# A graph-network kernel: basis loads on 96 partitions and 16-bit one-hots for sorting and counting the edges

## What is computed

```python
h = relu(layernorm(x))
x = x + L0(h, edges, node_vec1)      # 4 blocks of sparse attention and MLP, scale and bias of the norms from node_vec1
h = relu(layernorm(x))
x = x + L1(h, edges, edge_type_2)    # 2 relational layers

# attention of a block: softmax over the edges that leave a node
scores = sum(q[src] * k[dst]);  out = segment_sum(softmax(scores) * v[dst], src) @ wo + bo
# relational layer, R = 2 relations, B = 30 bases
w = einsum('rb,bio->rio', att, basis)                  # basis: 30 x 512 x 512
agg[row] += sigmoid(x[col] @ gate_w[r]) * x[col] @ w[r]     # r is the edge's type
out = agg + x @ root + bias
```

## Time and profile before

| | before |
|---|---|
| median of 3 executions | 2405.82 us (2404.52 to 2407.23) |
| profiled execution, its own time | 2413.9 us |
| its span | 2412.1 us |
| PE busy | 2200.1 us (91%) |
| PEld busy | 1886.1 us (78%) |
| DVE busy | 1638.5 us (68%) |
| ACT busy | 1153.2 us (48%) |
| POOL busy | 549.6 us (23%) |
| basis loads | 32 x 1920 KB, median 16.0 us from issue to landing |

### The profile page before, as it was taken

One profiled execution on the slowest core, in us unless ns is written; L12 is line 12 of the kernel. 1 busy time (PEld: TensorE's weight loads), 2 busy tenths in 40 slices (PEclk: granted clock), 3 DMA queues, 4 the chain that ended last, 5 costly groups with the idle time before them and its releaser, 6 DMA issues.

```text
span 2412.1 us, 36415 instructions
## 1 busy us (share of the span) xinstructions
PE 2200.1 (91%) x13669; PEld 1886.1 (78%) x13669; DVE 1638.5 (68%) x3599; ACT 1153.2 (48%) x1826; POOL 549.6 (23%) x402
## 2 busy tenths in 40 slices
PE   2678884899999999999999999999999999999999
PEld 1454443789988888998888999888899888877887
DVE  7989996548877646877754787765588775244234
ACT  4116668337773335775333777433477633322321
POOL 3400000016650003663000665100266400000000
PEclk9899996899999999999999999999999999999999
DMA  7699998211112202003101110320210231031023
GB/s 167 172 220 208 202 224 260 83 51 33 32 36 78 71 19 63 22 22 105 61 29 30 43 43 1 113 71 9 57 37 22 79 105 45 1 112 46 1 67 103
DMA packets 67182, 189.53 MB, mean 79 GB/s; under 512 B 6737, under 2 KB 7185, under 8 KB 66505
## 3 DMA queue, kind: packets, MB, share of 16 engines
q1 hardware_dynamic: 63318, 180.50, 28.0%
q10 hardware_dynamic: 3699, 6.76, 0.9%
HBM read 155.15 MB, written 32.07 MB: 78 GB/s over the span
## 4 chain that ended last, share of the span: by engine, by line
PE 70%; DVE 11%; issue 6%; ACT 6%; DVEq 3%; DMA 3%; SPq 1%; POOL 0%; ACTq 0%
PE PS L1039 10%; PE PS L1067 9%; PE PS L958 6%; PE PS L960 6%; PE PS L959 6%; PE PS L1053 6%; PE PS L944 5%; PE PS L948 4%; PE PS L945 4%; PE PS L1195 4%; PE PS L1205 4%; DVE chunk_hot L1660 2%; DVEq L1696 2%; ACT prob L1423 1%; PE PS L879 1%
## 5 line engine op out<-in xcount | busy, mean ns | idle before, releaser
L785 POOL TENSOR_SCALAR prob<-prob,inv_den 125x1000 f32<-125x1000 f32 x160 | 444.5, 2778 | 0.0
L773 POOL TENSOR_TENSOR rstd<-var_eps,neg_half 125x2 f32<-125x2 f32 x45 | 33.4, 743 | 954.6 <-DVE var_eps L1584 954.6
L1423 ACT ACTIVATE prob<-prob,neg_max 125x1254 f32<-125x1254 f32 x160 | 215.4, 1346 | 56.8 <-DVE neg_max L1916 56.6
L1911 DVE CUSTOM_DVE_ANT_0 prob<-PS,sbias 125x1254 f32<-125x1254 f32 x160 | 233.1, 1457 | 9.8 <-issue 7.1
L1067 PE MATMUL PS<-pT_hi,v_hi 125*128 125x250 f32 x800 | 236.1, 295 | 0.0
L1930 DVE TENSOR_TENSOR pT_lo<-PS,pT_hi 125x1000 fp32r<-125x1000 f32 x160 | 191.1, 1195 | 50.7 <-ACT pT_hi L1440 50.7
L1067 PE MATMUL PS<-pT_lo,v_hi 125*128 125x250 f32 x800 | 224.1, 280 | 0.0
L1067 PE MATMUL PS<-pT_hi,v_lo 125*128 125x250 f32 x800 | 222.4, 278 | 0.0
L1053 PE MATMUL PS<-ident,prob 125*125 125x125 f32 x1600 | 201.1, 273 | 5.6 <-DVE pT_lo L1933 5.6
L1053 PEld LDWEIGHTS PS<-ident,prob 125*125 125x125 f32 x1600 | 195.5, 188 | 12.7 <-issue 7.6
L1438 ACT ACTIVATE pT_hi<-PS 125x1000 fp32r<-125x1000 f32 x160 | 161.8, 1011 | 81.4 <-PE PS L1053 81.4
(11 more groups left out here) (329 smaller groups left out, 5725.2 us busy)
## 6 DMA issues: line engine op xcount, KB each, us to landing
basis_t<-in_L_gnn_basis_dram SPq DMA_DIRECT2D x32, 1920.0 KB, 16.0
sbias<-score_bias SPq DMA_DIRECT2D x40, 548.6 KB
adj<-adj SPq DMA_DIRECT2D x20, 546.9 KB
w_lo_raw<-in_L_gnn_m_w_dram SPq DMA_DIRECT2D x8, 1024.0 KB, 6.8
score_bias<-cnt SPq DMA_DIRECT2D x10, 548.6 KB
adj<-count_t SPq DMA_DIRECT2D x10, 546.9 KB
xc<-x_lat SPq DMA_DIRECT2D x12, 448.0 KB
x_first<-x_lat SPq DMA_DIRECT2D x10, 448.0 KB
```

Source lines behind the costliest of these rows:

```text
L785: pool.tensor_scalar(prob[u % 3][:, 0:SPLIT], prob[u % 3][:, 0:SPLIT], inv_den[0:T, u % 4:u % 4 + 1], None, ALU.mult)\
L1423: act.activation(prob[u % 3][:], prob[u % 3][:], ACT.Exp, bias=neg_max[0:T, u % 4:u % 4 + 1], accum_out=den[0:T, u % 4:u % 4 + 1]).then_in ...
L1911: v.tensor_tensor_reduce(prob[u % 3][:].rearrange("p (j s) -> p j s", j=3), PS[0:T, 0:3, 0:SB], sbias[p % 2][a][:].rearrange("p (j s) -> p ...
```

## The change

- `load_bases` brings 80 loads of 96 partitions (GROUP_B = 6 bases x GROUP_I = 16 rows) x 4 rows, 786 KB each, into RING = 6 buffers; a partition reads its four rows as 8 KB in one piece. Five loads (NBG) make one output bank of 128 rows, with four matmuls each, and `att_z` holds 5 blocks of 32 columns in place of shifted ones. The tables count loads now: 5 first, 2 and 3 in turn in the ten sort batches, one in each second group, one in the first bias tile.
- The sort has 10 batches of 16 chunks. `chunk_hot` is a single 16-bit compare per chunk and carries no code. For the whole batch one compare makes `place_hot` [128, 128 slots, 16 chunks], and two products make `src_place` and `dst_place` from it. PE multiplies each chunk_hot with both (two matmuls a chunk, banks 5 and 4); the stationary operand is `[:, :, i]`, with a step of 16 elements. DVE waits for `x_sums` once, since place_hot shares its bytes with ACT's `sq_junk`.
- `dst_hot` is made for two groups in one compare, [128, 128, 4]; its stationary slices have a step of 4 elements.
- The nine small loads move from SP's queue to ACT's, behind the ten loads of x.
- `load_r` brings each relation matrix in 8 pieces of 64 partitions.

```diff
-    QL = 8
-    SORT_BATCH = 8
+    GROUP_B, GROUP_I = 6, 16
+    NBG = B // GROUP_B
+    GP = GROUP_B * GROUP_I
+    GR = 4 * GROUP_I
+    RING = 6
+    SORT_BATCH = 16
...
-        STEPS_FIRST = 2 * QL
-        QUADS_SORT = [b for b in range(SORT_BATCHES) if b % 10]
-        QUADS_COUNT = [n for n in range(NG) if n % 8 in (1, 4, 7)]
+        LOADS_FIRST = NBG
+        LOADS_SORT = [2 + b % 2 for b in range(SORT_BATCHES)]
+        LOADS_COUNT = [n % 2 for n in range(NG)]
...
-                w = rel_w[l, :, n, :, :] if n < R else (root1, root2)[l].rearrange("(c p) d -> p c d", p=128)
-                sp.dma_start(wr_raw[n][:], w).then_inc(w_in[n].sem, 16)
+                if n == R:
+                    sp.dma_start(wr_raw[n][:], (root1, root2)[l].rearrange("(c p) d -> p c d", p=128)).then_inc(rel_in[n], 16)
+                else:
+                    for k in range(D // GR):
+                        p0 = GR * (k % 2)
+                        sp.dma_start(wr_raw[n][p0:p0 + GR, k // 2, :],
+                                     rel_w[l, k, :, :].rearrange("(j r i) d -> r i j d", j=4, r=R)[n]).then_inc(rel_in[n], 16)
...
             def load_bases(n):
-                l, q0 = divmod(n * QL, Q)
-                if n >= 3:
-                    sp.wait_ge(basis_used, n - 2)
-                rows = (basis1, basis2)[l].rearrange("b (i q k t) d -> (b i) q k t d", i=4, k=4, t=4)
-                t = q0 % 16 // 4
-                sp.dma_start(basis_t[n % 3][:].rearrange("p (k t) d -> p k t d", k=4),
-                             rows[:, q0 // 16, :, t:t + 2, :]).then_inc(basis_in[n % 3], 16)
+                group, g = divmod(n, NBG)
+                l, k = divmod(group, NW // 2)
+                if n >= RING:
+                    sp.wait_ge(basis_used, n - RING + 1)
+                rows = (basis1, basis2)[l].rearrange("(b g) a d -> g b a d", g=NBG)[g][:, GR * k:GR * (k + 1), :]
+                sp.dma_start(basis_t[n % RING][:], rows.rearrange("b (i j) d -> i b (j d)", j=4)).then_inc(basis_in[n % RING], 16)
...
+            def relation_loads(first, count):
+
+                for load in range(first, first + count):
+                    n, g = divmod(load, NBG)
+                    if g == 0 and n >= 2:
                         pe.wait_ge(basis_out, n - 1)
+                    pe.wait_ge(basis_in[load % RING], 16 * (load // RING + 1))
+                    for j in range(4):
+                        mm = pe.matmul(PS[32 * j:32 * (j + 1), 6 + n % 2, :],
+                                       att_z[n // (NW // 2)][:, g, :, :].rearrange("p r i -> p (r i)"),
+                                       basis_t[load % RING][:, j, :], start=(g == 0), stop=(g == NBG - 1))
+                    mm.then_inc(basis_used, 1)
...
-                    g = pe.matmul(PS[:, 5, 0:TC], place_hot[b % 2][:, i, :], chunk_hot[b % 2][:, i, :],
-                                  start=(c == 0), stop=(c == EC - 1))
+                    for bank, place in ((5, src_place), (4, dst_place)):
+                        g = pe.matmul(PS[:, bank, 0:TC], place[b % 2][:, :, i], chunk_hot[b % 2][:, i, :],
+                                      start=(c == 0), stop=(c == EC - 1))
                 g.then_inc(sort_used, 1)
...
-                        g = pe.matmul(PS[0:T, 3 * b + j, 0:SB], dst_hot[b][:, h, 0:T],
+                        g = pe.matmul(PS[0:T, 3 * b + j, 0:SB], dst_hot[n // 2 % 2][:, 0:T, 2 * b + h],
...
+            v.wait_ge(x_sums, 2 * NT + 1)
             for b in range(SORT_BATCHES):
...
-                    v.tensor_scalar(place_hot[b % 2][:, i, :], slot_no[:, 0:128], pos_p[:, c:c + 1], None, ALU.is_equal)
-                    last = v.tensor_scalar(chunk_hot[b % 2][:, i, :], slot_no[:], pos_c[:, c:c + 1], code[:, c:c + 1],
-                                           ALU.is_equal, ALU.mult)
-                last.then_inc(sort_hot, 1)
+                    v.tensor_scalar(chunk_hot[b % 2][:, i, :], chunk_no[:], pos_c[:, SORT_BATCH * b + i:SORT_BATCH * b + i + 1],
+                                    None, ALU.is_equal)
+                if b:
+                    v.wait_ge(sort_hot, b)
+                v.tensor_tensor(place_hot[:], by_slot(edge_place), slot_no[:], ALU.is_equal)\
+                    .then_inc(place_done, 1)
+                v.wait_ge(place_done, b + 1)
+                v.tensor_tensor(src_place[b % 2][:], place_hot[:], by_slot(edge_src), ALU.mult)
+                v.tensor_tensor(dst_place[b % 2][:], place_hot[:], by_slot(edge_dst), ALU.mult).then_inc(sort_hot, 1)
...
+                if b == 0:
+                    v.tensor_tensor(dst_hot[turn][:], slot_no[:, :, 0:4],
+                                    slot_dst[:, bass.ds(4 * it, 4)].unsqueeze(1).to_broadcast([128, 128, 4]), ALU.is_equal)
```

More of the change, by code:

```diff
@@ L826, in _ @@
             pe.wait_ge(att_ready, 2 * R)
-            relation_steps(0, STEPS_FIRST)
-            step = STEPS_FIRST
+            relation_loads(0, LOADS_FIRST)
+            load = LOADS_FIRST
             for b in range(SORT_BATCHES):
@@ L1510, in _ @@
                         o_high(4)
+                    if last and p in (0, 1, 3):
+                        r_high(0, (0, 1, None, 2)[p])
+                    elif p == 0:
                         w_high(wk_hi, wk_raw, 0, lay, 0)
```

241 lines of the change are left out of this document (115 added, 126 removed).

## The result

| | before | after |
|---|---|---|
| median | 2406.53 us (2404.52 to 2408.31) | 2364.73 us (2362.01 to 2368.22) |
| ratio, 95% interval | | 0.9829 (0.9816 to 0.9841) |
| profiled execution, its span | 2413.9, 2412.1 us | 2362.0, 2360.3 us |
| PE, DVE, ACT busy in the counting | 162.2, 191.4, 123.7 of 195 us | 178.4, 174.5, 123.4 of 179 us |

The account below looks back on a forecast made before the run. The prediction took VectorE to bound the setup's sort and counting, and ACT the bias tiles. Its terms, -25.5 - 1 - 15.7 - 3 + 2 = -43.2 us, gave a median of 2362 us, 8 in 10 within 2340 to 2400.

Parts of the forecast that it names:

- sort: Setup's sort: batched 16-bit one-hots and matmuls end it at 137.5 us instead of 163.0, saving 25.5 us.
- counting: Setup's counting: one compare serves two groups, 3.60 us per two groups on VectorE, 180.6 us in all, saving 15.7 us.
- bias tiles: Setup's ten bias tiles: fewer loads ahead of the store of adjacency counts, saving 3 us, between 0 and 11.
- behind: Relation weights at the end: 17 DMAs where 3 were, ahead of adjacency tile 2, costing 2 us, between nothing and 4.8.
- slot table: Table of slots in the setup: five instructions on 196 slots become two, saving 1 us.
- 24.2 us as a stop that remains: In the sort, POOL's z product and memset of count lock out VectorE for 24.2 us, before and after the change.
- The batch of 7.6 us on TensorE: In the sort, 32 matmuls at 0.16 us plus 2.5 basis loads at 0.99 take 7.6 us, over VectorE's 6.5.
- Rival D: POOL's lock in the sort shrinks, its product needing 2.88 us, not 13.47; 10 us more go: 2352 us, chance 0.14.
- Over 260 GB/s, then DMA hides: Setup's new basis loads run at over 260 GB/s, above the 242 needed in the counting, so their DMA is hidden.
- Rival A: Setup's basis loads stay slow at 205 GB/s, so 36 us of the saving go: 2398 us, chance 0.14.
- Rival B: Strided weights slow sort and counting; x, one matmul with its load, decides from 0.25 us: 2425 us, chance 0.10.
- Rival C: Two-input 16-bit compares with a repeated operand run at the 32-bit rate, 2.24 and 0.60 us: 2403 us, chance 0.06.

Follow-up runs that it names:

- e1: The kernel before, unchanged, profiled a second time: 2409.1 us, ratio 1.0001 to the kernel before, span 2403.1 us.
- e4: The changed kernel with the nine small loads back on SP's queue, behind the first six basis loads: 2367.8 us, ratio 0.9827.
- e3: The kernel before with the new basis loads and small relation-weight pieces, but its own sort, one-hots and small loads on SP's queue: 2404.8 us, ratio 0.9986.
- e7: As e6, with two basis loads in every sort batch and the five others in the bias tiles: 2361.1 us, ratio 0.9793.
- e2: The changed kernel with the old basis loads (32 loads of 120 partitions) and three DMAs for the relation weights: 2384.1 us, ratio 0.9887.
- e8: The changed kernel with dst_hot packed as 4 x 128, so its weights are read without a step: 2377.0 us, ratio 0.9854.
- e5: The changed kernel with layer 2's relation weights loaded behind adjacency tiles 2, 3 and 4 instead of ahead of tile 2: 2363.3 us, ratio 0.9802.
- e6: The changed kernel with count cleared on ACT in place of POOL's memset: 2358.3 us, ratio 0.9786.
- e11: The changed kernel with the six bases of a load 1 MB apart in HBM in place of 5 MB: 2367.5 us, ratio 0.9837.
- e10: The changed kernel with the edits of both e5 and e6: 2355.7 us, ratio 0.9784.

## Why the prediction was right

The number came out within 3 us of the median, but partly since errors cancelled: the sort was undersized by 6.8 us, and three other terms together (counting, bias tiles, behind) were too good by 7.0.

| term | forecast | by the spans against e1 |
|---|---|---|
| sort | -25.5 | -32.3 |
| slot table | -1 | -0.9 |
| counting | -15.7 | -13.4 |
| bias tiles | -3 | -1.3 |
| behind (relation weights) | +2 | +5.0 |
| sum | -43.2 | -42.9 |

**The sort.** The batch on VectorE was right: 6.41 us for 6.5. The step that failed inside the right sum is "24.2 us as a stop that remains". It was twice wrong: e1 shows 13.5 for the kernel before, so 163.0 was 8.4 us too late a base, and the changed kernel loses 10.6. So DVE has the second batch ready at 64.5 us, where the forecast had 74: 9.5 of the 15.2 us between 137.5 and 122.3. The other 5.7 come from TensorE: from there the forecast had 63.5 us to the end (nine batches of 7.6, less the short tail), and it took 57.8. Less the 8.4 of the base this makes the 6.8 by which the saving was undersized.

The batch of 7.6 us on TensorE went by 0.16 us a sort matmul. That holds at the lower clock (0.163 apart at 90.3 to 93 us) and not at the full one (0.085 at 121 to 122 us): 196 columns at 1.2 and 2.4 GHz. At full clock TensorE keeps up with VectorE, and until 90 us its batches start 6.41 us apart; the next two take 7.2 and 7.3 us, with matmuls of the noise net (2.3 us) and a stretch at the lower clock in them, and behind them a basis load is last. So TensorE as the limit was right for a part of the sort only, and the place near 122 us is the sum of three limits that no single term of the forecast had.

Rival D had the mechanism: POOL needs 2.8 to 6.0 us for the product in every other trace here, and the 13.47 with a chunk_hot of 10.8 us beside it occurred once. It was given 0.14 and should have had more, as the same shape stood in the profile with 2.88 us. But D put the gain at 10 us of time, and the median did not move with it, since the base moved too.

**The small loads** cost and bring nothing in the changed kernel (e4); the sum had no term of its own for them. But they were part of e1's 10.7 us wait on DVE, and e3 shows that the smaller basis loads ahead of them remove most of it without the move.

**The counting.** 3.60 us for two groups was exact, and the weight load stayed under the matmul, 196 ns under 203. Of the 2.1 us missing much is likely at the start: the three loads behind the last sort batch wait for DMAs until 128.9 us, and DVE then waits 3.2 us for PE, where e1 has 1.9 in all. That isn't shown to be all of it: in e7 no load waits there, and its counting is no shorter (183.8 us).

**The basis loads.** "Over 260 GB/s, then DMA hides" was half right: 257 to 269 with a full queue, enough in the counting, where PE waits for no load from 131 us on, not enough at the end of the sort. Rival A's mechanism is real where its condition holds (e2: 2384 us; A had put 2398), and the change avoids it.

**Rival B** is excluded: x was 0.085 to 0.163, its threshold 0.25. The Trainium skill (SBUF — State Buffer, Door 1: The DMA port swizzle) would let the 32-byte step of the sort pay and the 8-byte step of the counting go free. The rows say otherwise, the 8-byte step takes more: 145 to 154 ns in the sort (128x128), 196 in the counting and 136 packed (e8, both 128x125). **Rival C** is excluded by 1.22 us for a long compare and 0.34 for dst_hot; e8 shows that its rate of 0.60 is real for an operand whose step is 0 in the inner dimension.

**The end.** The term of +2 was undersized: it stood between nothing and 4.8 us, and PE waits 3.0 us. Neither of the two rules behind the bounds holds alone. A 64-partition piece takes 0.68 us to issue and not 0.43, so SP comes to the adjacency tile 8.8 us later than in e1 (11.6 us behind the first issue in place of 2.8); but the tile lands only 5.7 us later, and 2.8 of these were slack in e1. The other 1.7 us lie in the main part: at 490 to 510 us the granted clock is 0.92 where e1 has 1.00 at the same work. Its cause isn't shown. At that work the traces of before, e1 and e5 have 1.00, and the ten of the changed kernel, e2 to e4 and e6 to e11 have 0.86 to 0.93, e10 with the same edit as e5 among them; so the 1.7 us that e5 has back aren't shown to be the work of its edit.

**The bias tiles.** The chain still has the store of adjacency counts, 7.75 us (from 319.64) where it had 11.40 before. ACT itself waits for it once, 3.6 us (at 327.4 us), and waited 0.6 and 4.2 us before; that was worth 1.3 and not 3.

## What to carry to other kernels

Profile the base twice before a sum rests on it: one stop of two engines on each other made 8 us of difference between two profiles of the same kernel, more than several terms of this sum. When a faster loop asks for bytes more quickly, its gain and that of faster loads can't be priced apart. And count each small DMA that is put ahead of a load that someone waits for by the issue time of just that shape; here the tile came later by 5.7 of the 8.8 us that its issue did.
